# Loading and normalising the next token group from the start of a group's loop, and issuing its gate blocks ahead of the output projection

## What is computed

```python
x = x + attn(layernorm(x));  x = x + ffn(layernorm(x))

def attn(x):                     # gated linear attention, 16 heads of 64
    q, k, v = heads(x @ Wq.T), heads(x @ Wk.T), heads(x @ Wv.T)
    a = sigmoid(heads(x @ Wg.T))
    def step(h, inp):            # scan over the tokens
        q_t, k_t, v_t, a_t = inp
        h = a_t[..., None] * h + k_t[..., None] * v_t[..., None, :]
        return h, einsum('bhd,bhde->bhe', q_t, h)
    y = scan(step, zeros, (q, k, v, a))
    return layernorm(y, gamma, beta) @ Wo.T

def ffn(x):                      # integer weights times 1/127
    return (silu(x @ wg.T) * (x @ wu.T)) @ wd.T
```

## Time and profile before

| | us |
|---|---|
| median of three runs | 1528.4 |
| lowest and highest run | 1527.04, 1585.77 |
| the profiled execution, its time | 1529.17 |
| its span on the slowest core (core 6) | 1527.6 |
| spans of the eight cores | 1517.1 to 1527.6 |
| granted TensorE clock, mean of the cores | 0.817 to 0.820 |

### The profile page before, as it was taken

The page is one execution under the profiler, slowest core; times in us unless marked ns, Lnnn a source line. Parts: engine busy times, 40 slices in busy tenths (PEclk is TensorE's granted clock), DMA queues, the critical chain, the costliest instruction groups (busy, mean ns, idle before and its releaser), DMA issues.

```text
span 1527.6 us, 17799 instructions; the slowest of 8 cores (1517.1 to 1527.6 us)
## 1 busy us (share of the span) xinstructions
PE 945.6 (62%) x5892; PEld 446.2 (29%) x5892; DVE 514.4 (34%) x928; ACT 330.7 (22%) x691; POOL 136.6 (9%) x193
## 2 busy tenths in 40 slices
PE   0126376356572767436765300039999999999997
PEld 0004132222241323312333100014444444444443
DVE  0023245525653475616647544202221111111110
ACT  0033520542207320353102122101111111100000
POOL 2000000100001000100001000001101111101100
PEclk9967588678875878768976655569999999999999
DMA  9902200311124110321111145874334433403222
GB/s 143 164 25 74 42 0 8 111 42 49 41 43 110 36 49 14 91 63 55 42 29 50 62 131 125 159 107 42 34 36 42 42 38 32 56 28 111 97 97 97
DMA packets 144456, 99.97 MB, mean 65 GB/s; under 512 B 123504, under 2 KB 123504, under 8 KB 144368
## 3 DMA queue, kind: packets, MB, share of 16 engines
q0 software_dynamic: 72816, 81.02, 25.7%
q1 hardware_dynamic: 71552, 17.83, 6.0%
HBM read 93.86 MB, written 16.78 MB: 72 GB/s over the span
## 4 chain that ended last, share of the span: by engine, by line
PE 49%; DVE 16%; DMA 11%; ACT 10%; issue 6%; another core or an unknown queue 5%; SPq 1%; DVEq 1%; POOL 0%; ACTq 0%; POOLq 0%
PE p_g L888 11%; PE p_u L901 11%; PE p_d L927 11%; PE p_fr L336 4%; DMA s_x2T<-s_a 4%; DVE s_nL L357 3%; DVE s_nL L429 3%; DMA s_wd<-wdi 3%; PE p_py L469 2%; DVE s_ht L659 2%; DVE s_y L723 2%; ACT s_nL L261 2%; ACT s_nL L258 2%; PE p_fr L469 2%
## 5 line engine op out<-in xcount | busy, mean ns | idle before, releaser
L888 PE MATMUL p_g<-s_x2T,s_wgu 128*128 128x512 bf16 x768 | 183.1, 382 | 151.6 <-DMA s_wgu<-wui 151.6
L901 PE MATMUL p_u<-s_x2T,s_wgu 128*128 128x512 bf16 x768 | 182.1, 381 | 0.0
L336 PE MATMUL p_fr<-s_xlnT,s_wg 128*128 128x512 bf16 (+1 forms) x320 | 83.2, 424 | 142.8 <-DMA s_xlnT<-s_xln 128.0
L927 PE MATMUL p_d<-s_wd,s_hff 128*128 128x512 bf16 x768 | 165.9, 380 | 1.2 <-DVE s_hff L907 1.2
L907 DVE SCALAR_TENSOR_TENSOR s_hff<-p_u,s_act 128x512 bf16<-128x512 f32 x96 | 66.4, 692 | 293.5 <-PE p_u L901 293.5
L888 PEld LDWEIGHTS p_g<-s_x2T,s_wgu 128*128 128x128 bf16 x768 | 75.3, 98 | 243.5 <-issue 153.7
L894 ACT ACTIVATE s_act<-p_g 128x512 f32<-128x512 f32 x96 | 57.3, 597 | 270.8 <-PE p_g L888 270.8
L901 PEld LDWEIGHTS p_u<-s_x2T,s_wgu 128*128 128x128 bf16 x768 | 75.3, 98 | 91.5 <-issue 1.4
L927 PEld LDWEIGHTS p_d<-s_wd,s_hff 128*128 128x128 bf16 x768 | 75.0, 98 | 92.1 <-issue 1.7
L567 PE MATMUL p_pp<-s_wo,s_E 128*128 128x512 bf16 x256 | 81.6, 491 | 24.7 <-DVE s_xr L592 24.7
L336 PEld LDWEIGHTS p_fr<-s_xlnT,s_wg 128*128 128x128 bf16 x320 | 34.3, 112 | 190.3 <-issue 171.2
(11 more groups left out here) (109 smaller groups left out, 1132.9 us busy)
## 6 DMA issues: line engine op xcount, KB each, us to landing
s_x<-x2d POOLq DMA_DIRECT2D x32, 512.0 KB, 4.8
s_x<-xs POOLq DMA_DIRECT2D x18, 512.0 KB, 3.8
s_xr<-xs POOLq DMA_DIRECT2D x16, 512.0 KB, 3.4
x2d<-s_xr POOLq DMA_DIRECT2D x16, 512.0 KB, 2.9
out<-s_x POOLq DMA_DIRECT2D x16, 512.0 KB, 3.0
s_wd<-wdi POOLq DMA_DIRECT2D x1, 6144.0 KB, 43.3
s_wgu<-wgi POOLq DMA_DIRECT2D x24, 256.0 KB, 4.3
s_wgu<-wui POOLq DMA_DIRECT2D x24, 256.0 KB, 5.2
```

The source lines that it names most:

```text
L336: O.add("t", lambda t, p=p, j=j, bank=bank: t.matmul(p_fr[bank][:, 0:ntok], s_wg[:, 1024 * j + TILE * p:1024 * j + TILE * (p + 1)], s_xlnT ...
L888: addD("t", lambda t, buf=buf, t4=t4, j=j, pb=pb: t.matmul(p_g[pb][:], s_wgu[buf][:, TILE * j:TILE * (j + 1)], s_x2T[:, 2048 * j + 512 * t ...
L901: addD("t", lambda t, buf=buf, t4=t4, j=j, pb=pb: t.matmul(p_u[pb][:], s_wgu[buf][:, 1024 + TILE * j:1024 + TILE * (j + 1)], s_x2T[:, 2048 ...
L927: addD("t", lambda t, ts=ts, buf=buf, hf=hf, hcc=hcc: t.matmul(p_d[buf][:, 512 * hf:512 * (hf + 1)], s_hff[:, 2048 * hcc + TILE * ts:2048 ...
```

## The change

`emit_loads` is no longer one of the units. It is called at the start of `emit_loop`, right after the first two loads of s_xr, and for the first front directly. Its DMAs no longer wait for one another: only the first has a wait (the last layer norm that read s_x, of any tile), and one epoch closes behind all of them, so every layer norm waits for all of them.

The units of the other kinds keep their order. In a loop with four pairs the table is now `[5, 4, 4, 0]`, and the units are emitted before `emit_yln(w)` and `emit_be_late(w-1)` instead of after them; what is left behind the last pair (the scans) is emitted after `emit_be_late(2)`, as before. In the warm-up's loop the order stays as it was, apart from the loads.

```diff
--- before.py
+++ after.py
@@ -296,13 +296,16 @@
         x_eps = {}
 
         def emit_loads():
+            lw = [(SE, max([G["ln1_se"].get(tt, 0) for tt in range(nt)]))] + \
+                 ([(DQ, DQ.n)] if DEBUG else [])
             for tt in range(nt):
                 O.dma("g", SX, lambda g, tb=tb, tt=tt: g.dma_start(
                     out=s_x[:, 1024 * tt:1024 * (tt + 1)],
                     in_=xs.ap()[TILE * (tb + tt):TILE * (tb + tt + 1), :]),
-                    wait=[(SE, G["ln1_se"].get(tt, 0))] +
-                         ([(DQ, DQ.n)] if DEBUG else []))
-                x_eps[tt] = O.close_epoch(SX)
+                    wait=(lw if tt == 0 else ()))
+            ep = O.close_epoch(SX)
+            for tt in range(nt):
+                x_eps[tt] = ep
 
         def u_tile(tt):
             def run():
@@ -373,8 +376,11 @@
                 s_Er[:, 0:2048], s_nL[:, 0:2048], AF.Exp, scale=1.0), inc=SE)
             G["e0_done"] = SE.n
 
-        units = ([emit_loads] + [u_tile(tt) for tt in range(nt)] + [u_xt] +
-                 [u_gblk(p) for p in range(8)] + [u_scan0])
+        class _U(list):
+            pass
+        units = _U([u_tile(tt) for tt in range(nt)] + [u_xt] +
+                   [u_gblk(p) for p in range(8)] + [u_scan0])
+        units.loads = emit_loads
 
         def finish(dbg_this=False):
             s_done = SE.n
@@ -543,6 +549,8 @@
 
         xr_load(0)
         xr_load(1)
+        if splice:
+            splice.loads()
         vsg = {}
 
         def emit_vs(w2):
@@ -743,14 +751,24 @@
                 yt_eps[w] = O.close_epoch(YT)
                 G["yt_slot"][w % 2] = yt_eps[w]
                 emit_update()
+                if splice:
+                    sched = {4: [5, 4, 4, 0], 2: [6, 7]}[npair]
+                    for _ in range(min(sched[w], len(splice))):
+                        splice.pop(0)()
                 yst[w] = emit_yln(w)
                 G["yst_slot"][w % 2] = yst[w]
                 if w > 0:
                     emit_be_late(w - 1)
-            if par == 1 and splice:
-                sched = {4: [6, 4, 4, 9], 2: [7, 8]}[npair]
+                if splice and w == npair - 1:
+                    while splice:
+                        splice.pop(0)()
+            elif splice and wu and par == 1:
+                sched = {2: [6, 7]}[npair]
                 for _ in range(min(sched[w], len(splice))):
                     splice.pop(0)()
+                if w == npair - 1:
+                    while splice:
+                        splice.pop(0)()
             gc[0] += 1
 
         if not wu:
@@ -762,6 +780,7 @@
     ngrp = 0 if TRUNC in (1, 2) else (1 if TRUNC == 3 else 4)
     if TRUNC != 1:
         units, fin = prep_front(0, 2, True, 0)
+        units.loads()
         for u in units:
             u()
         FR = fin()
```

## The result

| | before | changed |
|---|---|---|
| median, us (10 and 9 runs) | 1529.35 | 1477.19 |
| ratio, 95% interval | 1 | 0.9651 (0.9634 to 0.9667) |
| profiled execution, us | 1529.17 | 1478.55 |
| span of the slowest core, us | 1527.6 | 1477.0 |

The forecast was 1453 us with a range of 1442 to 1469, so the time lies outside the range. The direction was right, the size was not: 52 us gained instead of 75.

What follows compares the result with a forecast made beforehand. Each loop was taken to be bound by the chain from the next group's loads through layer norms to landed transposes. Three loops at 25.1 us gave 75.3 us off the median 1528.4: 1453.1 us, range 1442 to 1469.

Steps and rivals of the forecast that it cites:

- the sum for a loop: Each of three loops feeding a next group: 24.9 + 0.7 - 0.5 = 25.1 us gained, 75.3 us for three.
- pair 1: Second pair of a loop: PE's wait for transposes nearly goes, mask starts at 480.9 instead of 505.82, 24.9 us gained.
- pair 2: Third pair of a loop: mask to mask takes 23.3 us instead of 24.02, 0.7 us gained.
- pair 3: Last pair of a loop: order as before, Y takes 1.85 instead of 1.33 us, 0.5 us lost.
- front: Scans, projections, stores and s_xr loads of a loop: follow as before, no change.
- the 7.25 us from the issue of the transposes to their use: SP to PE in a loop: four s_xln transposes issued from 456.3 are usable at 463.6, 7.25 us as before.
- if the four transposes take longer when the one of s_y flies ahead of them: Sign of being wrong, in the loops: the s_xln transposes are slowed behind the s_y one; no size given.
- Outside these three loops: Warm-up's loop, loop of group 3 and FFN: no gain or loss, all three 0.
- earlier loads change nothing: Warm-up's loop: norms start right behind an Exp and the last load was issued at 122.72, so 0 us.
- POOL against DVE's scans: Rival: early loads and scans hinder each other, scans up to 2.1 us longer per loop, 1459 us; chance 0.12.
- PE's clock: Two rivals on PE's matmul bursts: clock stays low, 1468 us, chance 0.15; clock high throughout, 1440 us, chance 0.06.
- The norms staying late: Rival: transposes land as now and the new order only costs, 8.0 us per loop, 1552 us; chance 0.04.

Runs made afterwards that it cites:

- e3: The kernel before with only the order changed, the loads still a unit of pair 0: 1548.4 us, ratio 1.0099.
- e4: The changed kernel with the units again behind the statistics of y and the output projection, only the loads early: 1549.2 us, ratio 1.0111.
- e1: The changed kernel, with the first of the four loads also waiting until the same group's s_xlnT transposes have landed: 1457.6 us, ratio to before 0.9523.
- e2: The changed kernel with the four early loads one after another, an epoch closed behind each: 1464.2 us, ratio to before 0.9567.
- e8: The changed kernel with the loads held behind the transposes in the warm-up's loop only: 1464.8 us, ratio to before 0.9576.
- e6: The changed kernel with loads held until the transposes land, and each pair ordered previous pair's projection, units, statistics of y: 1441.3 us, ratio to before 0.9366.
- e7: e6 with the statistics of y waiting only for their own pair's casts and state update, not the projection's DVE instructions: 1420.5 us, ratio to before 0.9279.
- e5: The changed kernel with each pair ordered previous pair's output projection, units, statistics of y: 1457.8 us, ratio to before 0.9493.

## Why the prediction was right and wrong

**Right: what bounds the loops, and that the wait goes.** The wait of 27 us per loop was a chain of loads, norms and transposes on three engines, and it fell to between 1.35 and 2.21 us. The list of waits was expected at about 46 us and shows 60.5, and the surplus lies in the two waits at the start.

**Right: both halves are needed.** The norms began right behind the Exp of the front (412.63), during the Q and K projections, as worked out, and e3 and e4 show that neither early loads nor the order alone brings this.

**Nearly right: the sum for a loop,** 25.1 us forecast. For the loop of group 1 (174.40 - 150.65 = 23.75 measured):

| term | forecast | measured | why |
|---|---|---|---|
| pair 1 | 24.9 | 22.8 | transposes usable 8.3 us after issue (450.52 to 458.83), not 7.25, and issued 0.1 later; PE's 48 matmuls took 13.0 us, not 12.2 |
| pair 2 | 0.7 | 1.1 | 22.92 us from mask to mask (477.07 to 499.99): PE's 48 matmuls took 10.9 us, not 12.2, but began 0.4 later, and the way from their end to the mask took 5.7, not 5.1 |
| pair 3 | -0.5 | -0.4 | 17.20 us from mask to scans, before 16.76 |
| front | 0 | 0.2 | 69.23 us, before 69.47 |

The pair 1 term is worked out from 42.5 us before (463.32 to 505.82) and 19.7 us after (the Y of pair 1 begins at 455.56, PE would have been free 1.85 us later, at 457.41, and the mask is at 477.07). The exposure of DVE's six instructions, 5.0 us, was as forecast. All three loops together gave 69.8 of 75.3 us. The largest term that was too small is the 7.25 us from the issue of the transposes to their use: it was 9.2, 8.3 and 9.1 us in the three loops, 4.9 us more in all. The prediction had named it as a sign of being wrong, "if the four transposes take longer when the one of s_y flies ahead of them". They took longer with it ahead of them; that it is the cause wasn't tried.

**Wrong: "Outside these three loops ... All three: 0".** The step that failed is in the sentence on the warm-up's loop: "earlier loads change nothing". It asked only whether the norms there would get their data sooner. It didn't ask what the loads would now stand beside. The same slip is in the term for group 0: its loads (for group 1) were moved from 278 to the moment at which the last norm of group 0's own tokens ends, which is exactly when SP issues the transposes that PE is waiting for. Both numbers that were needed were in the trace of before. The wait for the norm is written in the code (`ln1_se`). And the two transposes in the warm-up's front took 7.7 us there, beside one load, as long as the four in the front of group 0 with nothing beside them (7.3). The measured price is 7.1 us more than before at the first place, 7.9 at the second, and 1.4 us of small shifts between the runs. e1, e2 and e8 show it.

**The rivals.** POOL against DVE's scans: no price shows, but the contact was smaller than feared. The new loads are issued at 390.39 to 392.47, ahead of the scans at 394.54, which take 13.95 us, before 13.94; those of the next loop, at 544.06 to 546.14, reach 0.55 us into the scans at 545.59, which take 13.99. In both loops the loads land in about 8 us (median 7.8 and 7.9), so they aren't held to the end of the scans either. The Trainium skill's rule on the shared ports, page "SBUF — State Buffer", section "Who interferes with whom", that a VectorE instruction with two SBUF inputs collides with a GpSimd one that reads SBUF, agrees with these rows: the scans with two copies beside them take 13.95 us, those without 12.53. What four issues on top of the scans would cost, no run here shows. PE's clock: the 48 matmuls took 13.0 us in pair 1, at a granted clock of 0.80, and 10.9 us in pair 2 (483.44 to 494.30), at 0.96, where the sum had 12.2 for each. So neither rival on the clock was it, but one burst leaned to each of them, and it is luck that the two errors nearly cancel. The norms staying late: no.

The range was too narrow because it was made of the terms in the three loops alone. No bound was kept for moving 2 MB of loads in the two other loops, since the change there was taken to be nothing.

## What to carry to other kernels

When a transfer is made to start earlier, look up what releases it and what else the same event releases: a load that is needed 43 or 77 us later (the norms of its data begin at 155.15 and 258.96) can hold up a small transfer that is needed now, and a wait on that small transfer (e1) gave back all that the collision had cost and a little more. Go through the edit in every loop that runs the code, the short first ones too, and write down for each not only when the data is needed but what is in flight beside it. When instructions are reordered, read again what a wait that means "everything emitted so far" now includes.

## What the runs showed of the hardware

**Bulk loads in flight beside DMA transposes hold the transposes up, and the transposes lose most.** Four transposes of 128x1024 took 7.2 to 7.6 us from first issue to use with nothing beside them, 10.3 to 12.5 with one load of 512 KB at a time, 13.0 to 16.1 with four (all eight cores of e1, e2 and the changed kernel, second place). The four loads took 8.4 us (median to landing) beside the transposes and 7.3 without, and 9.1 and 7.7 us at the first place, so the waiting is not shared evenly. That the two meet on the 16 DMA engines fits their share of 0.85; no run separates it from another place at which they could meet.

**A pace of TensorE between its two levels.** The granted clock is at 0.50 where PE stood idle (the stretch 181 to 197 above) and at 1.00 in the FFN's matmuls. In the loops of e6, cores 0 to 3 did their large matmuls more slowly for a while. PE on core 2:

```profile
512.38 4.37 PE L476 MATMUL p_py<-s_xlnT,s_wq 128*128 128x512 bf16 x15
516.59 4.38 PE L476 MATMUL p_fr<-s_xlnT,s_wq 128*128 128x512 bf16 x16
520.79 4.37 PE L476 MATMUL p_pp<-s_xlnT,s_wq 128*128 128x512 bf16 x16
```

That is 4.21 us per 16, where the same code in e7 has 3.46 (starts at 500.72, 504.18 and 507.63). The granted clock over these rows is 0.81. The stretch 501 to 524 on cores 3 and 5 of e6, which also has the slow start of the V projection in it; the granted clock is the number ahead of the last two:

```profile
501.00:524.00 23.00, 22.86 (x80) 8.83 (x77) 13.30 (x34) 0.00 (x0) 5.07 (x8) 0.74 0.46 160
...
501.00:524.00 23.00, 18.84 (x80) 8.08 (x80) 15.20 (x38) 0.00 (x0) 5.75 (x9) 0.93 0.44 160
```

4.21 / 3.46 = 1.22. The Trainium skill, page "TensorE: Matmul & The Clock Gate", section "Seeing it yourself", names a peak-current limiter that holds a whole die to 13/16 of the clock, which would be 1.23. The ratio and the granted clock of 0.81 agree with it. That a whole die is held at once isn't shown here: cores 2 and 3 have the slow rows between 481 and 614, and cores 0 and 1 do the same projections in 3.45 us per 16 there; cores 0 and 1 have theirs one group earlier, between 337 and 470, where cores 2 and 3 do the projections in 3.45. Each core's times count from its own start, and how far apart the cores start no row tells. In the profiled e5 only cores 2 and 3 have such a run of rows, in e7 no core. What set it off wasn't tried: in the long dense stretch of the FFN (1100 to 1200) the granted clock of e6 was 1.00 on all eight cores.
